# A mixture-of-experts and Mamba kernel: new order of an expert's chunks, normalisation moved to ScalarE, the last chunk's back end by token halves

## Chip, cores and metric

One NeuronCore of a Trainium2 chip runs the kernel. The metric is device time in microseconds of one execution, median over runs; lower is better. Engines in the tables: PE is TensorE (PEld its weight loads), DVE VectorE, ACT ScalarE, POOL GpSimd, SP SyncE.

## The reference, cut to what matters

```python
x = x + 0.5 * ffn(layernorm(x))          # 4096 tokens of 256 values
x = x + attn(layernorm(x))
x = x + 0.5 * ffn(layernorm(x))

def ffn(h):                               # 8 experts, top 2, capacity 640 for each of the two choices
    probs = softmax(h @ gate_w.T + gate_b); topk_prob, topk_idx = top_k(probs, 2)
    for c in range(2):                    # a token behind the capacity is dropped
        pos = place of the token among those of its expert; keep = pos < CAP
        hmid = relu(xb @ W1[e] + b1[e])   # 256 -> 1024
        y += (hmid @ W2[e] + b2[e])[token] * (prob * keep)

def attn(x):                              # Mamba, 512 inner channels, 16 states, 2 sequences of 2048
    x = x + mamba(rmsnorm(x))
    h = square(relu(rmsnorm(x) @ c_fc_w.T))
    return x + h @ c_proj_w.T

def mamba(xn):
    x_in, z = split(xn @ in_proj_w.T)
    u = silu(causal_conv4(x_in) + conv_b)
    dt_low, B, C = split(u @ x_proj_w.T); dt = softplus(dt_low @ dt_proj_w.T + dt_proj_b)
    h[t] = h[t-1] * exp(dt[t] * A) + dt[t] * u[t] * B[t];  y[t] = sum_s(h[t] * C[t]) + u[t] * D
    return (y * silu(z)) @ out_proj_w.T
```

## The kernel before

The tokens stay in SBUF as `X`, 32 tiles of 128. The program is a chain of blocks with a barrier at each end: `route` for the first expert layer, `experts`, `mamba`, `route` and `experts` for the second. Inside a block each engine has a program written out by hand, and semaphores join them, so an engine's order is the order of its code.

**route.** In the first layer X comes in four quarters. VectorE takes each quarter's `statistics`, GpSimd the power that gives the reciprocal deviation (`rstd`) and, for some quarters, `shift`. TensorE turns the tokens and makes the gate's logits; ScalarE copies both from PSUM. VectorE then selects two experts a token for each half of the tokens (`chosen(0)`, `chosen(1)`), with exponentials by ScalarE in the middle of each. The normalised tokens are made in eight groups of four tiles: `norm(g)`, groups 0 to 4 on VectorE, 5 to 7 on ScalarE. SyncE stores each group to `xrows` in DRAM, then issues the loads of the first weights, the copies of X into `sums`, the small columns of weights (`halves`), and the second bias. Then slots and tables are made (`hot`, `inblock`).

**experts.** Each expert has up to 1280 rows, in five chunks (parts) of 256, so 40 chunks a layer, two experts a turn `i`. Parts 2 to 4 are computed only when the expert has that many rows (`if_taken`); where one isn't, its gathers, row splits, bias and scatters are still done. For each chunk GpSimd gathers the rows (two indirect DMAs of 128), TensorE turns them (L629), ScalarE and VectorE split them into a high and a low float (`xh`, `xl`), TensorE makes the product up in four pairs (48 products, L654), VectorE adds the bias, ScalarE and VectorE split the relu (`hh`, `hl`), TensorE makes the product down (48 products, L672), VectorE takes it from PSUM (L790), scales it, and GpSimd scatters it with two indirect DMAs that add (L583). In a step TensorE turns chunk c+2, makes up of c+1, then down of c. In steps 1 to 4 of an expert the next expert's weights are split, 1.2 us a step on VectorE. At the start TensorE makes `WARM` small bf16 products that nobody reads, behind the first indices.

**mamba.** Eight chunks of 512 tokens. `front` makes a chunk's inputs: T (turned rows), x (in projection), c (convolution of four channel tiles), xp (x projection), dt, sp (softplus), z. `turn` is the scan: 32 steps of two channel tiles, with two VectorE scans and one GpSimd product `dB` each; what belongs to the next chunk's front and the last chunk's back is hung into the steps by tables. `back` is out projection (`out`), squares (`sq`), root (`v`), scaled rows (`hr`), turned rows (`hT`), the forward layer (`fc`, `q`) and its projection (`pj`). A join (`out`, `pj`) is an identity product of 512 columns and eight products. In the tables all these share two PSUM banks. The first chunk's front runs alone ahead of the scan, the last chunk's back alone behind it, step by step over the whole chunk, and beside it VectorE and GpSimd make the second routing's statistics (`row_statistics`), normalised rows and selection: a `power` on GpSimd stands ahead of the back end's `v`. In the first front, channel tiles 2 and 3 are convolved by VectorE (`first_convolved`), 0 and 1 by TensorE with diagonal matrices.

## Time and profile before

| what | value |
|---|---|
| median of 3 runs | 1924.44 us (1921.66 to 1924.93) |
| profiled execution | 1920.51 us |
| its span, first to last instruction | 1918.7 us |
| mean granted TensorE clock | 0.925 of full |
| busy: PE, DVE, POOL, ACT | 1663.3, 1594.3, 1346.2, 1010.1 us |

Busy time is a sum over stages that have different limits. A "wait" row names who waited, for whom, the total, how often and the longest. In a timeline row the first number is the start, the second the time to the end of the last merged instruction, and the bracket the idle time before it with its releaser. Matmuls of fp32 stand in the profile twice, and they overlap, so their starts tell more than their lengths.

### The profile page before, as it was taken

The page shows a single profiled execution, that of the slowest core. Times are in us where ns is not written, and L with a number is a line of the kernel's source. Part 1 is how long each engine was busy: PE and PEld are TensorE (multiplying, and loading weights), DVE is VectorE, ACT ScalarE, POOL GpSimd, SP SyncE. Part 2 cuts the span into 40 slices and gives each one's busy share as a digit, 9 for nine tenths or more (in the row PEclk, how much of TensorE's full clock was granted, in tenths as well). Part 3 has the DMA queues.
Part 4 walks back from the last instruction along what each step waited for, and adds up shares of the span by engine and source line. Part 5 has one row for each costly group of instructions (what it writes and reads, how often), then busy time and mean ns, then how long its engine had stood idle before and what let it go on. Part 6 is the DMA issues. An engine that isn't in the chain of part 4 may idle for free. (4 is left out here: it accounts for less than half of the span.)

```text
span 1918.7 us, 31529 instructions
## 1 busy us (share of the span) xinstructions
PE 1663.3 (87%) x10960; PEld 1387.0 (72%) x10960; DVE 1594.3 (83%) x2694; ACT 1010.1 (53%) x1716; POOL 1346.2 (70%) x847
## 2 busy tenths in 40 slices
PE   6599999995777798989888899888795799999996
PEld 5599999994345556656565666656773699999996
DVE  7777777665699999999999999999996677677764
ACT  3433333331476768787776878777552533333331
POOL 2356555556498899998989999898951366565555
PEclk9699999997889799999989999999797799999998
DMA  5744444332544444443544444444424744443341
GB/s 179 191 122 93 81 94 90 80 70 32 196 140 170 144 153 151 148 163 129 173 133 152 156 154 141 146 161 148 153 67 131 189 89 98 90 91 81 80 72 22
DMA packets 161101, 237.62 MB, mean 124 GB/s; under 512 B 29482, under 2 KB 85408, under 8 KB 160416
## 3 DMA queue, kind: packets, MB, share of 16 engines
q1 hardware_dynamic: 130208, 198.84, 31.6%
q0 software_dynamic: 30720, 36.53, 11.6%
q8 instruction: 102, 1.67, 0.4%
q14 instruction: 71, 0.58, 0.1%
HBM read 202.57 MB, written 38.34 MB: 126 GB/s over the span
## 5 line engine op out<-in xcount | busy, mean ns | idle before, releaser
L1588 POOL TENSOR_TENSOR m_dB<-m_DTU,m_BC 128x1024 f32<-128x1024 f32 x256 | 601.8, 2367 | 42.4 <-DVE m_HS L1714 40.6
L1714 DVE TENSOR_TENSOR_SCAN PS<-PS,m_ST,m_dB 128x512 f32<-128x512 f32 x400 | 496.8, 1274 | 14.6 <-POOL m_dB L1588 14.0
L1331 ACT ACTIVATE PS<-m_DT,m_A 128x512 f32<-128x512 f32 x512 | 332.3, 682 | 160.2 <-DVE m_ST L1730 159.7
L1306 PEld LDWEIGHTS PS<-keep_ident,m_G 128*128 128x128 f32 x2048 | 254.7, 150 | 89.6 <-issue 55.1
L1306 PE MATMUL PS<-keep_ident,m_G 128*128 128x128 f32 x2048 | 284.6, 288 | 17.7 <-DVE m_G L1721 15.9
L713 ACT ACTIVATE e_hh<-e_u 128x512 fp32r<-128x512 f32 x252 | 156.2, 633 | 265.5 <-DVE e_u L771 258.8
L654 PE MATMUL PS<-e_xh,e_wh 128*128 128x256 f32 x1008 | 290.0, 288 | 3.0 <-DVE e_xl L750 3.0
L654 PE MATMUL PS<-e_xl,e_wh 128*128 128x256 f32 x1008 | 284.2, 282 | 0.0
L654 PE MATMUL PS<-e_xh,e_wl 128*128 128x256 f32 x1008 | 284.2, 282 | 0.0
L672 PE MATMUL PS<-e_wh,e_hh 128*128 128x256 f32 x1008 | 281.3, 279 | 0.0
L672 PE MATMUL PS<-e_wl,e_hh 128*128 128x256 f32 x1008 | 280.3, 278 | 0.0
L672 PE MATMUL PS<-e_wh,e_hl 128*128 128x256 f32 x1008 | 279.9, 278 | 0.0
L1721 DVE TENSOR_TENSOR m_G<-PS,m_BC 128x512 f32<-128x512 f32 x400 | 266.2, 672 | 7.0 <-PE PS L1306 6.9
L577 POOL DMA_INDIRECT e_xin<-xrows,e_gix x160 | 196.4, 1227 | 57.9 <-issue 44.2
L583 POOL DMA_INDIRECT out<-e_ysb,e_six x80 | 135.1, 1689 | 139.0 <-DVE e_ysb L795 121.3
L583 POOL DMA_INDIRECT sums<-e_ysb,e_six x80 | 136.3, 1703 | 131.4 <-DVE e_ysb L795 111.9
L790 DVE TENSOR_TENSOR e_ysb<-PS,layer_b 128x512 f32<-128x512 f32 x80 | 55.2, 690 | 170.5 <-PE PS L672 168.2
L654 PEld LDWEIGHTS PS<-e_xh,e_wh 128*128 128x128 f32 x1008 | 193.6, 192 | 3.7 <-issue 3.6
L654 PEld LDWEIGHTS PS<-e_xl,e_wh 128*128 128x128 f32 x1008 | 193.9, 192 | 0.0
L654 PEld LDWEIGHTS PS<-e_xh,e_wl 128*128 128x128 f32 x1008 | 193.2, 192 | 0.0
L672 PEld LDWEIGHTS PS<-e_wl,e_hh 128*128 128x128 f32 x1008 | 189.3, 188 | 0.0
L672 PEld LDWEIGHTS PS<-e_wh,e_hh 128*128 128x128 f32 x1008 | 189.2, 188 | 0.0
(262 smaller groups left out, 3169.2 us busy)
## 6 DMA issues: line engine op xcount, KB each, us to landing
m_BC<-bc_rows SPq DMA_DIRECT2D x512, 256.0 KB, 3.8
layer_raw<-w SPq DMA_DIRECT2D x64, 512.0 KB, 3.8
xrows<-r_xn SPq DMA_DIRECT2D x9, 512.0 KB, 3.5
keep_X<-x SPq DMA_DIRECT2D x4, 1024.0 KB, 9.6
sums<-keep_X SPq DMA_DIRECT2D x4, 1024.0 KB, 11.0
out<-keep_X SPq DMA_DIRECT2D x4, 1024.0 KB, 11.1
keep_X<-sums SPq DMA_DIRECT2D x3, 1024.0 KB, 15.2
e_xin<-xrows,e_gix POOLq DMA_INDIRECT x160, 3.2
```

What stands on the lines that cost most here:

```text
L577: G.indirect_dma_start(out=xin[:, c % CPE, t, :], out_offset=None, in_=xrows, in_offset=column(gix, c, t), bounds_check=last_token, oob_is ...
L583: G.indirect_dma_start(out=sums, out_offset=column(six, c, t), in_=ysb[:, c % CPE, t, :], in_offset=None, compute_op=ALU.add, bounds_check ...
L654: last = M(PS[:, B_S1 + pair, m * CH:(m + 1) * CH], a, r, start=(n == 0), stop=(n == len(terms) - 1))
L672: last = M(PS[:, B_Y + c % 2, t * D:(t + 1) * D], a, r, start=(n == 0), stop=(n == len(terms) - 1))
L713: A(hh[:, c % 2, 2 * pair:2 * pair + 2, :], u[:, pair, :, :], ACT.Relu).then_inc(hh_ok, 1)
L790: V.tensor_tensor(ysb[:, c % CPE, :, :], PS[:, B_Y + c % 2, :].rearrange("p (t d) -> p t d", t=CHT), b2.unsqueeze(1).to_broadcast([P, CHT, ...
L1306: last = M(PS[:, B_Y + j, ts], G[:, m % NG, j, ts], C["ident"][:, :], is_transpose=True, start=False, stop=(s == DS - 1 and m == n and a = ...
L1331: return nc.scalar.activation(out, in_, func, **kw)
L1588: G_.tensor_tensor(dB[:, at % NDB, :, :], DTU[:, es, :], BC[:, s % NBC, 0:1, :].to_broadcast([P, 2, CT]), ALU.mult).then_inc(dB_ok, 1)
L1714: V.tensor_tensor_scan(HS[:, on_pool_before(n) % 2, :] if on_pool(n, j) else state(n, j), state(n, j), dB[:, (k * STEPS + n) % NDB, j, :], ...
L1721: V.tensor_tensor(G[:, n % NG, j, :], state(n, j), BC[:, s % NBC, 1, :], ALU.mult).then_inc(g_ok, 1)
```

## The change

It has six parts.

1. `route`: only groups 1 and 3 are normalised by VectorE. ScalarE makes 0 and 2 between its copies in quarters 1 and 2, and 4 to 7 behind the second exponentials; the first exponentials stand behind the last quarter's first copies. GpSimd makes `shift` for all quarters. SyncE stores in the order 1, 0, 3, 2, 4 to 7.
2. `experts`: the part that a position computes is given by a table, (0, 1, 3, 2, 4) for the first expert of a layer and (3, 0, 4, 2, 1) for the others. The row count of the next expert is read one chunk earlier.
3. `experts`: GpSimd gathers two chunks further ahead (`LEAD`), and `down` waits for `hl` pair by pair instead of for all four.
4. Warm products: 72 instead of 40 in each expert layer, with 18 more behind the first transposes; 44 at the start of `mamba`, behind the first statistics.
5. First front of `mamba`: VectorE convolves tiles 2, 3 and 1, TensorE only 0; the x projection adds its terms in the order 2, 3, 0, 1, each as its tile is ready.
6. The last chunk's back end (`tail`): each step by two halves of 256 tokens, over eight PSUM banks.

Parts 1 to 3:

```diff
-        ON_ACT = (5, 6, 7)
+        ON_DVE, ON_ACT = (1, 3), (0, 2, 4, 5, 6, 7)
+        STORED = (1, 0, 3, 2, 4, 5, 6, 7)
...
                 statistics(0)
                 statistics(1)
-                norm(0)
                 norm(1)
                 statistics(2)
-                norm(2)
                 norm(3)
                 statistics(3)
                 dve.wait_ge(gb_in, 16)
                 chosen(0)
-                norm(4)
                 chosen(1)
...
-        WARM = 40
+        WARM = 72
+        LEAD = 2
+        FIRST_ORDER, ORDER = (0, 1, 3, 2, 4), (3, 0, 4, 2, 1)
+
+        def part(i, c):
+            return (FIRST_ORDER if (i, c // CPE) == (0, 0) else ORDER)[c % CPE]
...
-            j = c % CPE
+            j = part(i, c) % CPE
             if j < 2:
                 return work()
             eng.sem_inc(passed, 1)
-            with eng.If(rows > j * CH):
+            with eng.If(known[2 * i + c // CPE] > j * CH):
...
-                pe.wait_ge(hl_ok, i * (TURN * FP) + (c + 1) * FP)
+                pe.wait_ge(hl_ok, i * (TURN * FP) + c * FP + 1)
...
                     for n, (a, r) in enumerate(terms):
+                        if t == 0 and n % 6 == 0:
+                            pe.wait_ge(hl_ok, i * (TURN * FP) + c * FP + n // 6 + 1)
```

Parts 5 and 6, TensorE's side; ScalarE's and GpSimd's `tail` follow the same halves, with GpSimd's root(0), power(0), root(1), power(1):

```diff
-        ON_VECTOR = [("c", 2), ("c", 3)]
+        ON_VECTOR = [("c", 2), ("c", 3), ("c", 1)]
...
+        TAIL_ITEMS = [("out", 0, 0), ("out", 1, 1), ("hT", 0, 4), ("fc", (0, 0), 5), ("fc", (0, 1), 3), ("hT", 1, 4),
+                      ("fc", (1, 0), 0), ("fc", (1, 1), 1), ("pj", 0, 5), ("pj", 1, 3)]
...
+            def tail():
+                k = MCH - 1
...
+                for h in range(2):
+                    tail_joined("out", h, W_OUT, lambda e: T3[:, e:e + 1, :], XP[:, 2 * h:2 * h + 2, :])
+                pe.wait_ge(kept, MCH * STEPS)
+                tail_turned(0)
+                wait_read(pe, MCH, ("dt", 1), ("z", 3))
+                logits(5, PS[:, R_L[5], :]).then_inc(r_l, 1)
+                pe.wait_ge(r_xT, 1)
+                tail_forward(0)
+                tail_turned(1)
+                logits(6, PS[:, R_L[6], :]).then_inc(r_l, 1)
+                tail_read(pe, "out", 1)
+                tail_forward(1)
+                for h in range(2):
+                    pe.wait_ge(q_ok, k * 2 + h + 1)
+                    pe.wait_ge(xa_ok, k * 2 + (h + 1 + XA0))
+                    tail_joined("pj", h, W_PJ, hid, X[:, bass.ds(k * CTT + 2 * h, 2), :])
```

ScalarE in the first routing, from the third quarter's copies of turned rows (`r_xnT`) on; `r_lg<-PS` are logits, `r_lg<-r_lg` the exponentials, `r_xn` the normalised groups. Before:

```order
L381 ACTIVATE r_xnT<-PS 128x1024 x2
L384 ACTIVATE r_lg<-PS 128x32 x2
L369 ACTIVATE r_lg<-r_lg 128x128
L375 ACTIVATE r_xn<-keep_X,r_small 128x256 x4
L381 ACTIVATE r_xnT<-PS 128x1024 x2
L384 ACTIVATE r_lg<-PS 128x32 x2
L369 ACTIVATE r_lg<-r_lg 128x128
L375 ACTIVATE r_xn<-keep_X,r_small 128x256 x8
```

The same engine in the changed kernel, from the second quarter's copies on:

```order
L378 ACTIVATE r_xnT<-PS 128x1024 x2
L372 ACTIVATE r_xn<-keep_X,r_small 128x256 x4
L385 ACTIVATE r_lg<-PS 128x32 x2
L378 ACTIVATE r_xnT<-PS 128x1024 x2
L372 ACTIVATE r_xn<-keep_X,r_small 128x256 x4
L385 ACTIVATE r_lg<-PS 128x32 x2
L378 ACTIVATE r_xnT<-PS 128x1024 x2
L366 ACTIVATE r_lg<-r_lg 128x128
L385 ACTIVATE r_lg<-PS 128x32 x2
L366 ACTIVATE r_lg<-r_lg 128x128
L372 ACTIVATE r_xn<-keep_X,r_small 128x256 x16
```

Between the third and the fourth quarter's copies stand now only logits and one normalised group made ahead of them; four groups stand at the end.

TensorE behind the last scan, from the gated rows (`m_YT`) on; `m_XP` with `m_MW,m_TH` is `out`, `keep_gate` are logits, `m_XR` turned rows, `m_hT` forward, `keep_X` with `m_MW,m_TH` is `pj`. Before:

```order
L1177 MATMUL PS<-keep_ident,m_YT 128x128 x8
L1234 MATMUL PS<-m_XP,keep_ident 128x512
L1237 MATMUL PS<-m_MW,m_TH 128x256 x8
L1234 MATMUL PS<-m_XP,keep_ident 128x512
L1237 MATMUL PS<-m_MW,m_TH 128x256 x8
L1258 MATMUL PS<-keep_gate,m_XI 128x8 x8
L1258 MATMUL PS<-keep_gate,m_xrT 128x8 x8
L1242 MATMUL PS<-keep_ident,m_XR 128x128 x8
L1246 MATMUL PS<-m_hT,m_MW 128x512 x8
L1234 MATMUL PS<-keep_X,keep_ident 128x512
L1237 MATMUL PS<-m_MW,m_TH 128x256 x8
```

And in the changed kernel, from the second join of `out`:

```order
L1312 MATMUL PS<-m_XP,keep_ident 128x512
L1315 MATMUL PS<-m_MW,m_TH 128x256 x8
L1323 MATMUL PS<-keep_ident,m_XR 128x128 x4
L1294 MATMUL PS<-keep_gate,m_XI 128x8 x8
L1332 MATMUL PS<-m_hT,m_MW 128x256 x8
L1323 MATMUL PS<-keep_ident,m_XR 128x128 x4
L1294 MATMUL PS<-keep_gate,m_xrT 128x8 x8
L1332 MATMUL PS<-m_hT,m_MW 128x256 x8
L1312 MATMUL PS<-keep_X,keep_ident 128x512
L1315 MATMUL PS<-m_MW,m_TH 128x256 x8
```

The turned rows and the forward products come in two halves, and the two groups of logits, which stood together ahead of them, now stand between: one behind each half's turned rows.

## Rows read from the trace of the kernel before

**Rows 1.** Windows: busy time of each engine, TensorE's granted clock, DMA share, GB/s.

```profile
75.00:456.00 381.00, 370.97 (x3176) 369.67 (x3174) 274.57 (x506) 129.74 (x195) 224.75 (x167) 0.98 0.41 87
526.00:1423.00 897.00, 784.12 (x3838) 545.88 (x3838) 876.88 (x1183) 663.80 (x1144) 826.87 (x425) 0.93 0.44 149
```

**Rows 2.** The page's costliest groups: count, then busy us, mean ns, idle before.

```profile
L713 ACT ACTIVATE e_hh<-e_u 128x512 fp32r<-128x512 f32 x252 | 156.2, 633 | 265.5 <-DVE e_u L771 258.8
L654 PE MATMUL PS<-e_xh,e_wh 128*128 128x256 f32 x1008 | 290.0, 288 | 3.0 <-DVE e_xl L750 3.0
L654 PE MATMUL PS<-e_xl,e_wh 128*128 128x256 f32 x1008 | 284.2, 282 | 0.0
```

**Rows 3.** Waits of TensorE from 75 to 470 us: total, times, longest.

```profile
PE PS L629 <- DVE e_xl L750: 6.0, 2, 3.0
...
PE PS L629 <- DMA e_xin<-xrows,e_gix: 2.5, 1, 2.5
```

**Rows 4.** Window behind layer 0's first pair of left-out chunks: TensorE busy, granted clock, DMA.

```profile
124.90:132.30 7.40, 7.40 (x52) 0.77 0.79 205
```

**Rows 5.** Timeline of VectorE and GpSimd at the end of both expert layers.

```profile
455.52 0.69 DVE L790 TENSOR_TENSOR e_ysb<-PS,layer_b 128x512 f32<-128x512 f32 x1 [3.90 <-PE PS L672]
...
470.68 1.56 POOL L583 DMA_INDIRECT sums<-e_ysb,e_six  x1 [0.31 <-issue]
...
1899.96 0.69 DVE L790 TENSOR_TENSOR e_ysb<-PS,layer_b 128x512 f32<-128x512 f32 x1 [3.88 <-PE PS L672]
...
1903.95 1.54 POOL L583 DMA_INDIRECT out<-e_ysb,e_six  x1 [0.30 <-issue]
...
1911.37 1.54 POOL L583 DMA_INDIRECT out<-e_ysb,e_six  x1 [0.30 <-issue]
```

**Rows 6.** Scatters (L583) from 466 to 472 us, all of chunks left out.

```profile
DMA to landing us min/median/max: 2.7/2.7/2.7
```

**Rows 7.** Scatters (L583) from 1893 to 1898 us, of a computed chunk.

```profile
DMA to landing us min/median/max: 3.7/4.0/4.2
```

**Rows 8.** Timeline of ScalarE and VectorE in the first routing.

```profile
30.48 2.06 ACT L375 ACTIVATE r_xn<-keep_X,r_small 128x256 f32<-128x256 f32 x4
...
34.77 1.38 DVE L225 TENSOR_SCALAR r_xn<-keep_X,r_small 128x256 f32<-128x256 f32 x4
...
39.23 0.29 DVE L260 TENSOR_TENSOR r_lg<-r_lg,r_small 128x128 f32<-128x128 f32 x1 [3.07 <-ACT r_lg L384]
```

**Rows 9.** Timeline of SyncE's queue, its last issue in the first routing.

```profile
61.20 5.56 SPq L200 DMA_DIRECT2D layer_b<-b  x1
```

**Rows 10.** Waits of SyncE's queue up to 80 us.

```profile
SPq L204 <- DMA xrows<-r_halves: 5.9, 1, 5.9
SPq L109 <- PEq L109: 1.6, 1, 1.6
```

**Rows 11.** Windows with L654 alone: TensorE and weight loads busy, granted clock, DMA.

```profile
83.70:88.60 4.90, 4.89 (x24) 4.89 (x24) 0.54 0.44 91
88.60:91.80 3.20, 3.01 (x26) 2.82 (x24) 1.00 0.77 80
```

**Rows 12.** Timeline of VectorE and GpSimd in the first front of mamba.

```profile
497.77 0.49 DVE L1667 TENSOR_SCALAR m_U<-m_XI,m_mc 128x512 f32<-128x512 f32 x1 [4.78 <-ACT m_XI L1331]
...
500.54 0.48 DVE L1667 TENSOR_SCALAR m_U<-m_XI,m_mc 128x512 f32<-128x512 f32 x1
...
520.61 1.23 DVE L1675 TENSOR_TENSOR m_DT<-m_DT,m_XR 128x1024 f32<-128x1024 f32 x1 [2.73 <-ACT m_XR L1331]
...
518.02 2.90 POOL L1525 TENSOR_TENSOR m_tk<-m_tk,m_mhalf 128x16 f32<-128x16 f32 x1 [1.21 <-DVEq L1648]
...
523.25 11.60 POOL L1588 TENSOR_TENSOR m_dB<-m_DTU,m_BC 128x1024 f32<-128x1024 f32 x5
```

**Rows 13.** Timeline of TensorE and VectorE in the last back end.

```profile
1427.72 3.62 PE L1237 MATMUL PS<-m_MW,m_TH 128*128 128x256 f32 x16
...
1467.29 0.75 DVE L1748 BATCH_NORM_STATS2 m_SZ<-keep_X 128x6 f32<-128x256 f32 x2 [3.56 <-ACT keep_X L1331]
```

More of the change, by code:

```diff
@@ L183, in _ @@
                 sp.dma_start(C["b1"][:, :], b1).then_inc(setup_sem("b1_in"), 16)
-                for g in range(NG):
+                for g in STORED:
                     if g in ON_ACT:
@@ L591, in step @@
             def step(i, c, first=False, last=False):
-                if not (last and c + CPE >= TURN):
-                    gp.wait_ge(picked, i * TURN + (c + 1))
-                    gp.sem_inc(carried, 1)
-                    gather(i, c + CPE)
+                for ahead in range(LEAD + 1) if first and c == 0 else (LEAD,):
+                    read = c + ahead
+                    if not (last and read + CPE >= TURN):
+                        gp.wait_ge(picked, i * TURN + (read + 1))
+                        gp.sem_inc(carried, 1)
+                        gather(*((i, read + CPE) if read + CPE < 2 * TURN else (i + 1, read + CPE - TURN)))
                 if c % CPE == 0:
@@ L678, in _ @@
             turn(0, 0, first=True)
+            for _ in range(WARM // 4):
+                M(PS[:, B_Y + 1, 0:P], C["onesb"][:, :], C["upper"][:, :], start=True, stop=True)
             up(0, 0, first=True)
             def step(i, c, last):
-                if c % CPE == 0:
-                    rows[0] = rows_of(pe, i, c // CPE)
+                next_rows(pe, i, c, rows)
                 if not (last and c + 2 >= TURN):
@@ L1066, in run @@
             last_yz()
-            for p in BACK:
-                between(p)
-                back(p, MCH - 1, 1)
+            tail()
         def items(engine, n, k, par, has_front, has_back, front, back, rows=lambda p: None):
@@ L1157, in _ @@
             M = nc.tensor.matmul
+            pe.wait_ge(var_ok, 1)
+            for _ in range(WARM):
+                M(PS[:, B_H, 0:P], C["onesb"][:, :], C["upper"][:, :], start=True, stop=True)
             pe.wait_ge(w_in, 16)
@@ L1207, in front @@
                     pe.wait_ge(w_in2, 16)
-                    pe.wait_ge(u_ok, k + 1)
-                    for e in range(EK):
-                        last = M(bank(p, k, XPR), weights(W_XP, XPR, e, 0, XPR), U[:, par, e, :], start=(e == 0), stop=(e == EK - 1))
+                    order = (2, 3, 0, 1) if is_first(k) else range(EK)
+                    if not is_first(k):
+                        pe.wait_ge(u_ok, k + 1)
+                    for at, e in enumerate(order):
+                        if is_first(k) and ("c", e) in ON_VECTOR:
+                            pe.wait_ge(conv_silu, ON_VECTOR.index(("c", e)) + 1)
+                        elif is_first(k):
+                            wait_read(pe, k, ("c", e))
+                        last = M(bank(p, k, XPR), weights(W_XP, XPR, e, 0, XPR), U[:, par, e, :], start=(at == 0), stop=(at == EK - 1))
                 elif kind == "dt":
@@ L1272, in rows, with tail_joined @@
                 last.then_inc(written(p, MCH), 1)
-            def between(p):
-                if p == ("g", 2):
-                    for d in range(DK):
-                        last = rows_turned(6, d, PS[:, R_T[6] + d, :])
-                    last.then_inc(r_T, 1)
-                elif p == ("hT", 0):
-                    wait_read(pe, MCH, ("dt", 1), ("z", 3))
-                    logits(5, PS[:, R_L[5], :]).then_inc(r_l, 1)
-                    pe.wait_ge(r_xT, 1)
-                    logits(6, PS[:, R_L[6], :]).then_inc(r_l, 1)
+            def tail_joined(kind, h, at, src, rows):
+                out = tail_bank(kind, h)
+                M(out, C["ident"][:, :], rows.rearrange("p t d -> p (t d)"), start=True, stop=False)
+                for t in range(2):
+                    for e in range(EK):
+                        last = M(out[:, t * D:(t + 1) * D], src(e)[:, 0, (2 * h + t) * P:(2 * h + t + 1) * P],
+                                 weights(at, D, e, 0, D), start=False, stop=(t == 1 and e == EK - 1))
+                last.then_inc(f_w, 1)
@@ L1308, in turn @@
                         last.then_inc(g_read, 1)
-            run(pe, turn, front, back, lambda: None, between)
+            run(pe, turn, front, back, lambda: None, tail)
             for h in range(2):
-                wait_read(pe, MCH - 1, ("pj", h))
+                tail_read(pe, "pj", h)
                 if h == 0:
@@ L1512, in _ @@
+            run(act, turn, front, back, lambda: None, tail)
             for h in range(2):
@@ L1564, in power, with tail, root @@
                                  ALU.pow).then_inc(r_pow, 1)
-            def between(p):
-                if p == ("v", 0):
-                    power(0)
-                    power(1)
+            def tail():
+                k = MCH - 1
+                def root(h):
+                    own = ssq[:, 2 * h:2 * h + 2]
+                    gp.wait_ge(sq_ok, k + h + 1)
+                    G_.tensor_tensor(own, own, eps[:, 0:2], ALU.add).then_inc(v_ok, 1)
+                    gp.wait_ge(v_ok, k + h + 1)
+                    G_.tensor_tensor(own, own, mhalf[:, 0, 0:2], ALU.pow).then_inc(rs_ok, 1)
+                root(0)
+                power(0)
+                root(1)
+                power(1)
+                for h in range(2):
+                    tail_read(gp, "out", h)
+                    x = X[:, bass.ds(k * CTT + 2 * h, 2), :]
+                    G_.tensor_tensor(x, x, XP[:, 2 * h:2 * h + 2, :], ALU.add).then_inc(xa_ok, 1)
             def weigh(k, n):
@@ L1599, in last_products @@
                         weigh(MCH - 1, n)
-            run(gp, turn, front, back, last_products, between)
+            run(gp, turn, front, back, last_products, tail)
             power(2)
@@ L1662, in first_convolved @@
                 dve.wait_ge(tail_ok, 1)
-                for n in range(2, EK):
+                for n in (e for _, e in ON_VECTOR):
                     wait_read(dve, 0, ("x", n))
```

165 lines of the change are left out of this document (122 added, 43 removed), and 2 rows, old and new, of the table base.

## Prediction

> **What bounds the kernel now.** I read the stages first, then who waited for whom inside them, then single rows. The two expert layers are bound by TensorE: from 75 to 456 us it is busy 370.97 of 381 us at a granted clock of 0.98. The scan from 526 to 1423 us is bound by VectorE, busy 876.88 of 897 us [rows 1]. The change leaves the steady part of both as it is: the same products, scans and transfers per chunk. What it can win lies in the seams: the first routing, the first chunk of each expert layer, the places where chunks are left out, the end of each expert layer, and both ends of the mamba stage. So each seam is priced by what ends last in it.
>
> Which chunks are left out matters for most of it. ScalarE's row L713 stands 252 times, four to a chunk that is computed, so 63 of the 80 chunks run [rows 2]. The lengths of the steps between TensorE's transposes (L629) show which: in layer 0 part 4 of experts 1 and 3, parts 3 and 4 of experts 0 and 6, parts 2 to 4 of expert 7; in layer 1 the same, but expert 7 leaves out only 3 and 4.
>
> **Chunks left out (c).** Where two neighbours are left out, TensorE has only transposes to do and waits for the split of the next rows: two waits of 3.0 us in layer 0 [rows 3], and two such in layer 1. Behind the first of them the clock is granted at 0.77 over 7.4 us of work, so some 1.6 us more is lost [rows 4]; one of the two in layer 1 shows the same, the others do not. The new order (3, 0, 4, 2, 1) puts computed chunks between parts 3 and 4, so four stalls of 3.0 us and two slow stretches of some 1.6 us go. Three things come back. Expert 7 of layer 0 leaves out parts 4 and 2, which are neighbours now: one wait stays, about 1.9 us, since the weight split of 1.2 us inside the old waits is missing in the last expert. A computed chunk between two that are left out has no other products behind which VectorE can make its low halves. That would cost some 2 us each, but the products down now start on the first pair and wait pair by pair; I take 0.3 us for each of six places, and 0.6 us for the last chunk of layer 0. Layer 0: -7.6 + 1.9 + 1.5 = -4.2. Layer 1: -7.6 + 0.9 = -6.7. **Sum -10.9**, bounds -15 and -5. The added waits themselves: in the products up, where each pair has a wait already, the term that begins a pair lasts 288 ns and the next 282 [rows 2]. 1008 times 6 ns over 252 waits is 24 ns a wait, so three more in each of 63 chunks cost at most 4.5 us. I take nothing, since these rows hold the slow first chunk too, and keep 4.5 as the bound.
>
> **Ends of the expert layers (d).** In layer 0 VectorE takes the last computed chunk from PSUM at 455.52. Then GpSimd issues eight scatters, six of them for chunks that are left out, the last from 470.68 to 472.24. In layer 1 it is 1899.96 and 1912.91. A chunk's own two scatters end 5.5 us after VectorE's read (1903.95 plus 1.54 against 1899.96) [rows 5]. In the new order the last position is always part 1, which is computed, so only these 5.5 us follow TensorE: 16.7 becomes 5.5 in layer 0, 12.95 becomes 5.5 in layer 1. Against it: a scatter that writes nothing lands in 2.7 us [rows 6], one that writes in 4.0 [rows 7], and issues some 0.3 longer. Layer 0: -11.2 + 1.6 = -9.6. Layer 1: -7.4 + 1.6 = -5.8. **Sum -15.4**, bounds -18 and -12.
>
> **First routing (a).** Three groups of four normalisations, 1.38 us each, leave VectorE for ScalarE, two of them ahead of its first selection. ScalarE's exponentials and its norm(5) (30.48, 2.06 us) stood ahead of the last turned rows, and so VectorE got its last logits only at 39.23, after 3.07 us of idle [rows 8]. Now the last quarter's copy comes first: it ends near 29.3, and the logits are there near 32.5. VectorE's first selection is held for its exponentials to about 29.65, one us sooner than before, and ends at 33.85, where the second starts: 5.4 us sooner. But the stage has a second chain. SyncE's last issue ended at 66.76 [rows 9], its wait for the small weight columns lasted 5.9 us more, to 72.6, and then it waited 1.6 us for the others [rows 10]. This chain hangs on the last normalised group, as all stores are issued before the sums. ScalarE makes that group behind the second exponentials, which come 5.4 sooner, but with two more groups of 2.06 ahead of it: 1.3 sooner. So SyncE ends at 71.3 and the stage, before at 74.2, with it: **-2.9**, bounds -1.3 and -5.4.
> The Trainium skill (Trainium Architecture — The Big Picture, The five engines, in one table) says that ScalarE is not for simple arithmetic, VectorE being up to about three times as fast per element. The row here shows a factor of 1.5, so the measurement decides. An estimate from that page's factor: four groups of 4.1 us behind the second exponentials would end 8 us later than mine, and the stage would cost 5 us instead of giving 2.9.
>
> **First chunk of each layer (b).** The warm products now number 72, with 18 more behind the first transposes. Before, the 40 ended 2.5 us ahead of the gathered rows [rows 3], and the first 24 products ran at a granted clock of 0.54 in 4.89 us; the next 24, with transposes, took 3.0 at full clock [rows 11]. So 2.2 us go, and 0.4 in the first transposes: **-5.2** for both layers. 72 products at the slow rate last about as long as the gather, so they delay nothing much. Bounds +1 (clock not raised, warm products late) and -6.5. VectorE's second pair of weight splits still ends before the second chunk's rows, so its chain moves along.
>
> **Front of mamba (e).** A third channel tile on VectorE costs 2.77 us (497.77 to 500.54). It takes c1 from TensorE, so the x projection ends some 4.4 us sooner. But VectorE still has three statistics blocks between its convolutions and the first sum of DT at 520.61, and GpSimd's power at 518.02 for 2.90 us hangs on the last of them, with the first dB at 523.25 behind four factors [rows 12]. All of this moves back by 2.77, of which some 1.4 returns, since two of GpSimd's factors took a us each beside VectorE's sums and now run alone: +1.35. If the 44 warm products raise the clock for the x products, these are 2.9 us earlier, and the front gains 1.5. I take **0**, with these two as bounds.
>
> **Last back end (f).** Before, the power of the row statistics stood ahead of the squares' root, out(1) waited for a bank, the whole chunk passed from step to step, and VectorE got the last rows at 1467.29. A join is 3.62 us of products and 0.9 for its identity term [rows 13]. By halves: out(0) and out(1) end at 1431.3 and 1435.85; squares, root and scale of the first half pass under out(1), and scaled rows stand at 1437.4. Transposes and logits(5) last to 1440.0, forward(0) to 1443.6, transposes and logits(6) to 1446.1, forward(1) to 1449.7, both joins to 1458.7, the copy to 1459.4: 7.9 sooner. Price: logits(6) come behind forward(0), so VectorE's selection starts 0.5 us later, and ScalarE's exponentials stand ahead of its next forward copy, 0.3 us; VectorE has reached the last statistics by 1457.5, so neither is on the chain. **-7.8**, bounds -9 and -4.
>
> **Sum.** -2.9 - 5.2 - 10.9 - 15.4 + 0 - 7.8 = -42.2. The profiled execution took 1920.5 (span 1918.7), which gives 1878.3; the median of the runs lies 3.9 above it: 1882. A difference of 0.2%, 3.8 us, is about what a measurement of this kernel can tell from none.
>
> **Rivals.**
> *Clock and stores.* The warm products don't hold the full level (the first 40 had lost it before their rows came [rows 11]) and the routing ends on its stores. Without b, without the 3.2 us of slow stretches in c, and with a at -1.3: -32, or 1892. Chance 0.2.
> *Every seam at its good bound:* the routing's transfers shrink with its chain, the x products find the full clock, left-out chunks cost nothing: -50, or 1874. 0.12.
> *The order does not do what it says.* If each left-out chunk still lets TensorE run dry, c is 0, and if the last scatters wait for one another's landing at the end of the layers, d halves: -24, or 1901. For it: every double left-out place shows its wait; against it: no wait of TensorE for a single left-out chunk stands beside them [rows 3]. 0.08.
> *GpSimd's power shuts VectorE out.* The sum of DT would begin behind the power, at 523.75, and the first dB at 526.3, 3.0 later than before instead of 0: 1885. Before, the sum began 0.3 us before the power ended and took 1.23 us as its neighbour did [rows 12]. 0.05. The Trainium skill (SBUF — State Buffer, SBUF: two separate sides) states this as a lock on a shared port pair, held for a whole instruction.
> *Slower: the finer waits open a bubble in every chunk.* TensorE is the bound through both layers, so each of the 63 computed chunks pays in full. From 42.2 / 63 = 0.67 us a chunk, 0.22 a wait, the gain is gone; at 0.3 a wait the time is 1939. The begun pairs bound it at 0.024 [rows 2]. 0.03. Within 0.2% of before: 0.02.
> The forecast itself has 0.5, with a range of 1877 to 1888. The whole range reaches into the neighbours: 1873 to 1897. All but the last two cases are faster: 0.95.
>
> **What would show it.** Right: no wait of 3.0 us on e_xl, but one near 2 in layer 0; two scatters behind TensorE's last product in each layer; VectorE's last logits of the routing without idle before them, and SyncE the last to end that stage; the first 24 products in 2.7 us; VectorE's last statistics of the mamba stage 7.8 us nearer to its last scan. Wrong: a first dB that lies later behind layer 0's last scatter than 51 us by more than 3; products down with gaps at each pair; more than one slow stretch in a layer.

## The result, and the profile after

The changed kernel takes 1879.6 us (median of four runs, 1878.3 to 1883.6) against 1924.4 for the kernel before: ratio 0.977, 95% interval 0.976 to 0.979. The forecast was 1882 with a range of 1873 to 1897. The profiled span falls from 1918.7 to 1877.9, by 40.8 us; the medians differ by 44.8, because the profiled execution of the kernel before took 3.9 less than its median. The ledger below cuts both traces at the same events, so its rows add up to the 40.8. "Read" is VectorE taking a chunk's result from PSUM.

| stretch | before | after | gain | forecast |
|---|---|---|---|---|
| a: start to first turned rows | 81.21 | 77.23 | 4.0 | 2.9 |
| b: first to third turned rows, both layers | 10.62 + 11.02 | 8.19 + 8.15 | 5.3 | 5.2 |
| c: from there to the read of the last computed chunk, layer 0 | 363.69 | 361.51 | 2.2 | 4.2 |
| c: the same, layer 1 | 375.25 | 370.04 | 5.2 | 6.7 |
| d: from that read to the mamba stage; to the end | 22.65; 18.74 | 12.36; 12.23 | 16.8 | 15.4 |
| e: start of mamba to first dB | 45.08 | 43.61 | 1.5 | 0 |
| scan, first dB to last product | 898.65 | 899.80 | -1.2 | 0 |
| f: to the last statistics | 45.39 | 38.32 | 7.1 | 7.8 |
| from there to the first turned rows of layer 1 | 46.40 | 46.46 | -0.1 | 0 |

The waits of TensorE in layer 0 (78 to 465 us; columns: total, how often, longest). Two waits of 3.0 us on e_xl stood here [rows 3]; one of 2.4 is left, at expert 7. Its row names VectorE's branch past a left-out chunk (L551), which VectorE reaches right behind its split of the rows:

```profile
PE PS L668 <- DVEq L551: 2.4, 1, 2.4
PE PS L668 <- DVE e_xl L765: 0.5, 1, 0.5
```

The page's groups of the products. In the products down the first group holds the products that begin a pair, a quarter of its 1008. Its mean is 281 ns where the other terms take 278, and it has 0.2 us of idle time in all. Before, it was 279 and 278. In the run with the old order below, which keeps the pair waits, it is 279 again, so the waits by themselves cost nothing that can be seen:

```profile
L688 PE MATMUL PS<-e_wh,e_hh 128*128 128x256 f32 x1008 | 283.3, 281 | 0.2
L688 PE MATMUL PS<-e_wl,e_hh 128*128 128x256 f32 x1008 | 280.5, 278 | 0.0
```

The end of layer 0, from GpSimd's timeline (start, length, bracket: the idle time before). Behind VectorE's last read, at 446.93, only two scatters begin and not eight [rows 5], once the one that began at 446.87 is over:

```profile
449.07 1.57 POOL L595 DMA_INDIRECT sums<-e_ysb,e_six  x1 [0.64 <-issue]
450.94 1.56 POOL L595 DMA_INDIRECT sums<-e_ysb,e_six  x1 [0.30 <-issue]
```

Windows of the start of layer 0: the first 24 products run at the full granted clock in 2.9 us, where they took 4.89 at 0.54 [rows 11]:

```profile
79.30:82.25 2.95, 2.91 (x25) 2.94 (x26) 2.51 (x3) 1.06 (x2) 2.41 (x2) 1.00 0.33 52
82.25:85.42 3.17, 3.17 (x30) 3.17 (x29) 1.88 (x5) 0.90 (x2) 2.56 (x3) 1.00 0.54 120
```

The first routing: SyncE's waits, and the timeline of VectorE and GpSimd. The second selection starts at 32.72 without idle time, 6.5 us sooner than before [rows 8]. SyncE then ends the stage with its wait for the small columns, and GpSimd's first indices stand at 70.56 (before, 74.62):

```profile
SPq L205 <- DMA xrows<-r_halves: 6.2, 1, 6.2
```

```profile
32.72 0.29 DVE L261 TENSOR_TENSOR r_lg<-r_lg,r_small 128x128 f32<-128x128 f32 x1
...
70.56 0.19 POOL L577 COPY e_gix<-layer_token 128x10 uint32<-128x10 uint32 x1 [26.53 <-POOLq L109]
```

The last back end, TensorE's timeline and a window. The same 16 forward products take 5.39 us for the first half of the tokens and 3.69 for the second, and the granted clock of the first stretch is 0.69:

```profile
1418.04 0.63 PE L1323 MATMUL PS<-keep_ident,m_XR 128*128 128x128 f32 x4 [1.57 <-ACT m_XR L1408]
...
1420.21 5.39 PE L1332 MATMUL PS<-m_hT,m_MW 128*128 128x256 f32 x16
...
1427.95 3.69 PE L1332 MATMUL PS<-m_hT,m_MW 128*128 128x256 f32 x16 [0.23 <-ACT m_hT L1408]
```

```profile
1420.00:1425.50 5.50, 5.50 (x21) 4.53 (x21) 5.50 (x11) 1.41 (x3) 4.80 (x3) 0.69 0.61 191
```

### The profile page after: what moved, and what is told of

It is laid out like the page before. It is cut to its first block and busy times, and to the rows that moved or that the text cites. A ratio compares the mean times of both kernels' runs of the same rounds, so it can differ in the third digit from the quotient of the medians.

```text
span 1877.9 us, 31848 instructions
## 1 busy us (share of the span) xinstructions
PE 1657.1 (88%) x11110; PEld 1388.6 (74%) x11112; DVE 1591.0 (85%) x2686; ACT 1014.9 (54%) x1728; POOL 1341.7 (71%) x851
## 5 line engine op out<-in xcount | busy, mean ns | idle before, releaser
L1858 DVE TENSOR_TENSOR_SCAN PS<-PS,m_ST,m_dB 128x512 f32<-128x512 f32 x400 | 498.6, 1281 | 15.4 <-POOL m_dB L1732 14.8
```

What stands on the lines that cost most here:

```text
L1858: V.tensor_tensor_scan(HS[:, on_pool_before(n) % 2, :] if on_pool(n, j) else state(n, j), state(n, j), dB[:, (k * STEPS + n) % NDB, j, :], ...
```

## The experiments

Every kernel is the changed one with the edit shown. Where a ratio stands, it is against the kernel before. Gains and losses are read between the events of the ledger.

### The order of the chunks

```diff
-        FIRST_ORDER, ORDER = (0, 1, 3, 2, 4), (3, 0, 4, 2, 1)
+        FIRST_ORDER, ORDER = (0, 1, 2, 3, 4), (0, 1, 2, 3, 4)
```

> The changed kernel, but every expert computes its chunks in the order 0, 1, 2, 3, 4 again; finer waits, warm products and the rest stay. The profiled changed kernel has a span of 1877.9 us. By my ledger of the two traces the two expert layers gained 7.4 us between their third transposes and their last computed chunk, and 16.8 us behind it. Theory A, the order makes both: waits of 3.0 us on e_xl stand again at the doubled left-out places, eight and six scatters behind the last computed chunk; span about 1902. Rival B, a good part comes from reading row counts and gathering two chunks further ahead, and from the pair waits: the waits of 3.0 us stay away and only the end comes back, span about 1895.

Measured: 1905.2 us, ratio 0.991 (0.989 to 0.992), span 1904.0. TensorE's waits on e_xl at the left-out places of layer 0 are those of before:

```profile
PE PS L643 <- DVE e_xl L765: 6.0, 2, 3.0
PE PS L668 <- DVE e_xl L765: 0.5, 1, 0.5
```

Stretch c is 363.58 and 375.01 us, as before (363.69 and 375.25), and d is 22.48 and 18.61. So the order makes all of c and d, 23.5 us of the 26.1 between the spans; the rest lies in the first routing (1.2) and the scan (1.3). Theory A holds. Reading the row counts sooner, gathering further ahead and waiting pair by pair are worth nothing by themselves, and the pair waits cost nothing either: the group of products down that holds them takes 281.2 us here and took 281.3 before, and stretch c is as long as before to 0.3 us.

```diff
-        FIRST_ORDER, ORDER = (0, 1, 3, 2, 4), (3, 0, 4, 2, 1)
+        FIRST_ORDER, ORDER = (0, 1, 3, 2, 4), (0, 2, 3, 4, 1)
```

> The changed kernel with the order 0, 2, 3, 4, 1: the last position is computed, as in the change, but parts 3 and 4 (and 2 where it is left out) are neighbours again. The first expert of a layer keeps 0, 1, 3, 2, 4. Tells the end of a layer apart from the stalls. If the stalls are what the new order removes beside the end: layer 0 has one wait of 3.0 us at expert 6 and two at expert 7 in place of the one of 2.4, layer 1 one at expert 6 and one at expert 7; 9.6 us more, less 0.9 for isolated places that go, and up to 1.6 us for each slow stretch behind a wait: span 1886 to 1891, with the ends of both layers as short as in the change (18.9 less 0, the mamba stage starting 12.4 us behind VectorE's last read). Rival: the ends lengthen too, because the scatters of left-out parts queue up ahead of the last: then span above 1893.

Measured: 1895.0 us, ratio 0.986 (0.984 to 0.987), span 1893.7. The span is 2.7 us above the range of the first theory and in that of the rival, but not for the rival's reason: the ends are as short as in the change (12.32 and 12.48), so a computed last position is all that d needs. Stretch c is 371.64 and 374.14, 10.1 and 4.1 us longer. In layer 0 the expectation had 6.6 and up to 1.6 for each slow stretch. TensorE waits in four places, one at expert 6 and three at the three left-out neighbours of expert 7 (columns as above). The wait for the split of the weights (e_wl) was not foreseen, and behind the others the granted clock falls, to 0.79 over the 8 us behind the wait of expert 6 and to 0.70 from 440.6 to 452 us:

```profile
PE PS L643 <- DVE e_xl L765: 4.5, 2, 2.8
PE PS L668 <- DVEq L551: 2.9, 1, 2.9
PE PS L688 <- DVE e_wl L761: 2.1, 1, 2.1
```

### The wait for the low halves

```diff
-                pe.wait_ge(hl_ok, i * (TURN * FP) + c * FP + 1)
+                pe.wait_ge(hl_ok, i * (TURN * FP) + (c + 1) * FP)
...
-                        if t == 0 and n % 6 == 0:
-                            pe.wait_ge(hl_ok, i * (TURN * FP) + c * FP + n // 6 + 1)
```

> The changed kernel, but the product down waits for all four low halves at once, as before. Theory A: in places where TensorE has no products up of another chunk in between (left-out chunks on both sides, and the last chunk of each layer) it now stands until VectorE has made the fourth low half, about 2 us for each of six isolated places and two ends less what they cost already (0.3 to 0.6 us each): span 10 to 13 us longer, about 1889. Rival B: VectorE is early enough even there: within 1 us of 1877.9. Rival C: the pair waits cost 24 ns each in the ordinary chunk, so that taking them away gives back up to 4.5 us of this.

Measured: 1904.9 us, ratio 0.990 (0.988 to 0.992), span 1902.8. Stretch c is 13.6 us longer in layer 0 and 10.2 in layer 1: 23.8 us, about twice what theory A gave. The waits are where A put them, layer 0 first, then layer 1:

```profile
PE PS L686 <- DVE e_hl L789: 9.3, 4, 2.5
...
PE PS L686 <- DVE e_hl L789: 7.2, 3, 2.5
```

That is 16.5 us at seven places: six isolated ones and the last chunk of layer 0. In the change the same places cost 0.2 to 0.7 us each, read from the length of their steps. Some 7 us come on top of the waits, and the granted clock is the reason: over some 8 us it is 0.77 to 0.80 behind five of the seven waits and 1.00 behind two. The five steps lose 3.6 to 5.0 us against the change (the longest, of the last chunk, has a second slow stretch in it), the two others 2.1 and 2.4. Windows of two of them: the step with the first wait takes 10.38 us at a granted clock of 0.84, where the change takes 6.36 at 1.00: 2.5 us are the wait, and 1.5 the clock behind it. The other keeps the clock and loses 2.1 (6.56 in the change).

```profile
110.28:120.66 10.38, 7.88 (x55) 7.65 (x54) 5.86 (x12) 3.64 (x5) 8.07 (x7) 0.84 0.49 103
395.17:403.84 8.67, 6.35 (x54) 6.12 (x53) 4.80 (x11) 2.69 (x4) 6.55 (x6) 1.00 0.52 79
```

What follows: the order and the pair waits belong together. With the new order and the old wait, c is 11.4 and 5.0 us longer than before the change. With the old order the pair waits are worth nothing.

### The warm products

```diff
-        WARM = 72
+        WARM = 40
...
-            for _ in range(WARM // 4):
+            for _ in range(0):
...
-        WARM = 44
+        WARM = 0
```

> The changed kernel with 40 warm products in each expert layer, none behind the first transposes, none in the mamba stage. Theory A, the warm products hold the granted clock: the first 24 products of each layer take 4.9 us again instead of 2.7 and the two steps after the first transposes 10.6 and 11.0 us instead of 8.2, so 5.3 us more in the expert layers; in the mamba front the x products take 9.4 us instead of 7.1 and the first scan comes 2 to 3 us later. Span about 1886. Rival B: gathering further ahead made the first steps shorter and the clock is worth less: under 3 us in the expert layers.

Measured: 1888.7 us, ratio 0.982 (0.980 to 0.984), span 1889.4. First to third turned rows: 10.46 and 10.99 us, as before (10.62 and 11.02), so the warm products make all of b (5.1 us). From the start of mamba to the first dB it is 46.35 us, 2.7 more than in the change. The x products take 9.65 us there and 7.13 in the change:

```profile
479.50 9.65 PE L1222 MATMUL PS<-m_xrT,m_MW 128*128 128x512 f32 x16 [0.69 <-ACT m_xrT L1408]
```

```profile
473.52 7.13 PE L1222 MATMUL PS<-m_xrT,m_MW 128*128 128x512 f32 x16 [0.74 <-ACT m_xrT L1408]
```

The rest of the 11.5 us between the spans lies in the first routing (1.5), the scan (1.4) and stretch c (0.7), which this edit doesn't touch. Theory A holds for both places. Without warm products the front is 1.3 us slower than before the change (46.35 against 45.08), so something else in it costs time. The front has two more edits, the third channel tile and the order in which the x projection adds its terms; the next run takes the tile back.

### The front of the mamba stage

```diff
-        ON_VECTOR = [("c", 2), ("c", 3), ("c", 1)]
+        ON_VECTOR = [("c", 2), ("c", 3)]
...
+             (("c", 1), 3),
```

> The changed kernel with two channel tiles convolved by VectorE as before (2 and 3), and 0 and 1 by TensorE; the warm products of the mamba stage and the x projection in ready order stay. From the start of the mamba stage to the first dB: 45.08 us before, 43.61 in the change, 46.35 in the change without warm products. Theory A, the third tile costs 1.27 us (46.35 less 45.08) because VectorE's statistics and GpSimd's power behind them set the first dB: 42.3 now, 1.3 shorter than in the change. Rival B: TensorE's second convolution delays the x projection and with it DT: 43.6 or more. The earlier reading of which chain ends last is what it tests.

Measured (one profile): span 1875.8, first dB 41.40 us behind the start of the stage, 2.2 sooner than in the change, where nine profiles with three tiles lie between 43.5 and 43.9. With two tiles VectorE waits 1.14 us for ScalarE before the sum of DT, so ScalarE's side now ends last there. Rival B, which gave no gain at all, falls. Two rows of VectorE, the first of this kernel, the second of the change:

```profile
499.44 1.22 DVE L1819 TENSOR_TENSOR m_DT<-m_DT,m_XR 128x1024 f32<-128x1024 f32 x1 [1.14 <-ACT m_XR L1408]
```

```profile
499.27 1.29 DVE L1819 TENSOR_TENSOR m_DT<-m_DT,m_XR 128x1024 f32<-128x1024 f32 x1
```

With three tiles ScalarE has DT 5.2 us ahead of VectorE, which still makes statistics. The third tile is a loss, 2.2 us here. The new order of the x projection was not taken back, so what it gives is not shown. The scan is 898.8 us in this kernel and 899.0 to 901.2 in ten profiles with three tiles; before, it was 898.65. The nearest two are 0.2 us apart, so that a link with the tiles is not shown, and how they could lengthen the scan was not found.

The next kernel attacks the same wait from the other side:

```diff
-            for call in range(2, len(CALLS)):
+            for call in range(2, len(CALLS) - 1):
                 statistics(call, *CALLS[call])
             first_dt()
+            statistics(len(CALLS) - 1, *CALLS[-1])
...
+                        if is_first(k) and n == 3:
+                            factors(len(CALLS) - 1, *CALLS[-1])
```

> The changed kernel, but in the front of the mamba stage VectorE makes the sum and the product of the first DT ahead of its last statistics block, and GpSimd that block's factors behind the first four dB. In the change ScalarE has DT ready 34.8 us behind the start of the stage and VectorE starts its sum at 39.98, behind the statistics; with two tiles on VectorE the pair is 38.3 and 38.3, and the first dB stands at 41.40 instead of 43.61. Theory A, with three tiles on VectorE the statistics block of 4.9 us is all that stands between: sum at 35.1, first dB at 38.8, when GpSimd's power for the block before is done, first scan about 42.6 instead of 46.07, and nothing is given back, as VectorE waited there; span 1873 to 1875. Rival B: GpSimd's factors among the first dB delay the scan by 3.5 us, and the gain is gone.

Measured (one profile): span 1877.4. The first dB stands at 38.9 us, as worked out, 4.7 sooner than in the change. All of it is lost behind: the first scan comes 47.6 us behind the start of the stage (46.07 in the change). Rival B is not the reason, as GpSimd's factors come only at 511.4. The scan starts behind VectorE's small operations of the late statistics, and some of these stand while GpSimd makes dB. VectorE first, then GpSimd:

```profile
500.07 0.16 DVE L1784 TENSOR_TENSOR m_var<-m_st 128x8 f32<-128x8 f32 x1
500.16 2.32 DVE L1785 TENSOR_TENSOR m_var<-m_st 128x8 f32<-128x8 f32 x1
502.51 2.26 DVE L1786 TENSOR_SCALAR m_tk<-m_tk 128x8 f32<-128x8 f32 x1
504.80 0.17 DVE L1787 TENSOR_TENSOR m_var<-m_var 128x8 f32<-128x8 f32 x1
...
497.76 6.97 POOL L1732 TENSOR_TENSOR m_dB<-m_DTU,m_BC 128x1024 f32<-128x1024 f32 x3
```

An operation of 0.17 us takes 2.32, as long as one dB (6.97 / 3), and the next one waits out another dB. With the last dB over, 0.17 is back.

### The first routing

In the first of three kernels the small columns are issued right behind the normalised groups; in the second the copies into `sums` go ahead of group 4; the third has the routing of before.

```diff
+            if x_dram is not None:
+                weights_out()
             for q in range(4):
                 load_quarter(sp, W1, W2, raw, 0, q)...
```

```diff
                 for g in STORED:
+                    if g == 4:
+                        copy_sums()
```

> The changed kernel, but in the first routing SyncE issues the small weight columns right behind the normalised groups, ahead of the loads of weights and the copies of X into sums. In the changed kernel VectorE's last table stands at 67.2 us, SyncE's wait for these columns ends at 70.1, and the first indices at 70.56 (71.65 to 72.03 in four variants with the same routing). Theory A, SyncE's queue of stores ends the stage: the columns land some 15 us earlier, the wait for them goes, and the indices stand at 68.2 to 68.7, 2.0 to 3.5 us sooner; span about 1875.5. Rival B: something else (the copies into sums, b2's 1 MB, the barrier) ends within 0.5 us of it, and the stage ends at 70 or later.

> The changed kernel, but SyncE issues the four copies of X into sums (4 MB) ahead of the last four groups of normalised rows instead of behind the weights. SyncE waits 11.5 us there for ScalarE, and the DMA engines move nothing from 30 to 35 us, while from 45 to 70 us their share is 0.95 to 1.23. With the small columns issued first (the earlier run) the stage did not end sooner, as the copies then ended last. Theory A, the transfers as a whole end the stage, and filling the hole takes this chain away: first indices at 68.0 to 69.0, about 1 us behind VectorE's last table at 67.2, against 70.56 to 72.06 in seven profiles; span 1874 to 1877. Rival B: the stores of the last groups and the weights now queue behind the copies and end as late as before: 70 or later.

> The changed kernel with the whole routing stage as before (groups 0 to 4 normalised by VectorE, the old order of ScalarE and of the stores). Before, the first indices stood at 74.62; with the change at 70.56 in one profile and between 70.69 and 72.47 in seven others of the same text (one of them with another order of SyncE's queue). Theory A: the change of the routing is worth 2.2 to 4.1 us, first indices at 74.6 here, and nothing else moves; span about 1881. Rival B: part of the four microseconds is how one execution differs from another: indices at 73 or sooner.

Measured (one profile each): first indices at 72.06, 68.61 and 75.31 us, spans 1881.0, 1875.5 and 1883.9. Theory A of the first falls. The small columns no longer end last, but the copies into `sums` do, in SyncE's waits:

```profile
SPq L109 <- DMA sums<-keep_X: 6.5, 1, 6.5
```

So the place of the small columns in the queue was not it; the transfers as a whole are what is left. The second run shows it. Windows of 30 to 35 us, the change first (the last two columns are the DMA share and GB/s): the hole is filled. Two rows of the second run show VectorE's table of tokens and, 0.9 us behind it, the first indices; VectorE's last operation of the stage ends between them, at 68.25.

```profile
30.00:35.00 5.00, 1.29 (x12) 1.10 (x10) 4.14 (x16) 1.19 (x4) 0.00 (x0) 0.99 0.00 0
```

```profile
30.00:35.00 5.00, 1.80 (x17) 1.60 (x15) 4.18 (x15) 0.88 (x4) 0.00 (x0) 1.00 1.04 338
```

```profile
67.71 0.24 DVE L331 TENSOR_TENSOR layer_token<-layer_dest,r_masks 128x80 uint32<-128x80 uint32 x1
...
68.61 0.19 POOL L583 COPY e_gix<-layer_token 128x10 uint32<-128x10 uint32 x1 [24.08 <-POOLq L109]
```

The third run sizes term a. The old routing gives 74.62 and 75.31 in two profiles; the new one lies between 70.56 and 72.47 in nine, mean 71.4. So a is worth 3.6 us on average, and the 4.0 of the first profile is at its good end.

### The last back end

```diff
                 pe.wait_ge(kept, MCH * STEPS)
+                for _ in range(24):
+                    M(tail_bank("hT", 0)[:, 0:P], C["onesb"][:, :], C["upper"][:, :], start=True, stop=True)
                 tail_turned(0)
```

> The changed kernel with 24 small bf16 products that nobody reads in the gap of 1.57 us that TensorE has in the last back end ahead of its first turned rows (1416.5 to 1418.04). Behind that gap the clock was granted at 0.69 from 1420.0 to 1425.5 and the first half's forward products took 5.39 us, the second half's 3.69. Theory A, the gap (and the thin logits behind it) drops the clock, and the last back end is 7.1 us shorter than before instead of 7.8 for that reason: forward products of the first half in 3.7, VectorE's last statistics 36.6 us behind its last scan product instead of 38.32; span about 1876. Rival B: the slow stretch comes from the logits' thin products alone and stays: 38.3.

Measured (one profile): span 1876.8, last statistics 36.56 us behind the last scan product instead of 38.32. Theory A holds: the gap dropped the clock, and the thin logits behind it alone don't. TensorE's timeline and the window of the forward products, now at a granted clock of 1.00:

```profile
1416.06 1.50 PE L1349 MATMUL PS<-keep_upper,keep_onesb 128*128 128x128 bf16 x24
...
1419.90 3.70 PE L1332 MATMUL PS<-m_hT,m_MW 128*128 128x256 f32 x16
```

```profile
1420.00:1425.50 5.50, 5.50 (x37) 5.04 (x36) 5.50 (x11) 2.99 (x6) 4.56 (x3) 1.00 0.61 191
```

Of these 1.76 us, 0.8 are lost again behind them. From the last statistics to layer 1's first turned rows it takes 47.3 us here and 46.4 to 46.5 in every kernel without this edit; the last kernel below, which has it too, takes 47.2. Layer 1's first indices come 2.0 us sooner than in the change, but TensorE waits 1.61 us for the rows that they gather, and not 0.42. From 1479 to 1481 us, when the gather is issued, the DMA share is 0.56; in the change, at the same distance from its gather (1481 to 1483), it is 0.00. So other transfers, which did not move along, are likely what holds the gather up; no run tests it. TensorE's first turned rows, in the change and in this run:

```profile
1487.48 0.66 PE L643 MATMUL PS<-keep_ident,e_xin 128*128 128x128 f32 x4 [0.42 <-DMA e_xin<-xrows,e_gix]
```

```profile
1486.30 0.66 PE L643 MATMUL PS<-keep_ident,e_xin 128*128 128x128 f32 x4 [1.61 <-DMA e_xin<-xrows,e_gix]
```

### Gathering further ahead

```diff
-        LEAD = 2
+        LEAD = 0
```

> The changed kernel with gathers no further ahead than before (LEAD 0 instead of 2). In the prediction this edit has no term. Theory A, it only matters where steps are short (left-out chunks), where GpSimd's scatters and gathers of two chunks would fall into 6 us: up to 1 us at each of the eight left-out places of layer 0, span 0 to 5 us longer. Rival B: the gathers are needed: TensorE's transposes wait for DMA at each left-out place, over 10 us longer. Rival C: nothing, within 1 us.

Measured (one profile): span 1877.4. Stretch c is 361.23 us in layer 0 (361.51) and 369.56 in layer 1 (370.04). The edit is worth nothing that one profile can show, as rival C has it.

### The three findings together

The kernel holds three diffs from above: the copies into `sums` ahead of group 4, the 24 products in the last back end, and two tiles on VectorE.

> The changed kernel with the three edits that the runs point to: the copies into sums issued in SyncE's idle time, 24 small products in the gap of the last back end, and two instead of three channel tiles on VectorE in the first front. One by one they gave in the profiles: first indices at 68.61 instead of 71.4 (the mean of nine profiles of the changed routing), 1.76 us in the last back end, and 2.2 us at the first dB with about 0.7 more in the scan. If they add, 2.8 + 1.8 + 2.9 = 7.5 us: a span of 1871 to 1873 and a median near 1873, 0.973 to 0.975 of before. Rival: they overlap, as the granted clock or the phase of the products moves with every shift: 1876 or more.

Measured: 1873.4 us, ratio 0.974 (0.972 to 0.975), span 1871.6. First indices at 68.63, first dB 41.28 us behind the start of its stage, scan 898.51, last back end 36.57. Against the change that is 1.9 us at the indices, 2.3 at the first dB, 1.3 in the scan and 1.75 in the back end, less 0.7 lost behind it. The rest cancels, and the spans differ by 6.3. The time lies in the range that was expected, though two terms are smaller than there: the change's own profile has its first indices at the good end, and the loss behind the back end was not seen. The interval lies below that of the changed kernel (0.976 to 0.979), so this version beats both.

## Why the prediction was right

**The whole.** 42.2 us were forecast and the spans give 40.8. The terms are off by 0.1 to 3.5 us, in both directions, so part of the closeness is luck: a, d and e gave 4.0 us more than forecast, c, f and the scan 5.4 less. The forecast of 1882 rests on the 3.9 us between the profiled execution and the median before; the change showed no such distance (1879.7 and 1879.6).

**a.** The steps held: VectorE's last logits without idle time, SyncE last. Average 3.6, forecast 2.9. But the reason for SyncE's place was only half seen. The prediction hung its chain on the last normalised group; what ends it is the sum of the transfers behind, which an idle stretch of the DMA engines could have taken. ScalarE made four groups in a row in 7.96 us, 2.0 each as the row of before had it. The Trainium skill (Trainium Architecture — The Big Picture, The five engines, in one table) has ScalarE up to three times slower at simple arithmetic; the estimate made from that, a stage 5 us longer, does not hold here.

**b.** Right in size and cause: 5.3, and 5.1 of it goes with the warm products.

**c.** The mechanism was right, the size was not: 7.4 instead of 10.9. The stalls and slow stretches of left-out neighbours went as priced; what comes back is larger. The wait left at expert 7 is 2.4 and not 1.9 us. The isolated places cost 0.2 to 0.5 us in layer 0 as assumed, and 1.2 to 1.6 in all in layer 1 instead of 0.9. The rest is the pace of the products, below: more of them ran at the slower of two paces, some 2.5 us in both layers together. The order as such could not have won that. What the prediction priced well without seeing its weight is the pair waits: "some 2 us each" was 2.4, and a slower clock behind some of them would have made it 23.8 us in all.

**d.** 16.8 instead of 15.4, since the writing scatters cost 0.9 us more at each end and not 1.6. Of this price the 0.3 for the issue was misread: an issue takes 1.54 to 1.57 us whether its rows are written or not.

**e.** The forecast of 0 lay between two bounds, and the good one, 1.5, is what came. Both of its parts were real: a loss by the third tile (bound 1.35, measured 2.2 with warm products; the 1.27 without them holds the new order of the x projection too) and a gain by the clock (2.7 at the first dB; the x products gained 2.3 and not 2.9). The parts don't add up simply: with two tiles, the clock and the new order of the x projection give 3.7 us together. The chain was named rightly, VectorE's statistics; but the gain of the clock was kept out of the likeliest case. That GpSimd's power would shut VectorE out did not happen: the sum took 1.29 us beside it (before 1.23 [rows 12]).

**f.** 7.1 instead of 7.8. The step that failed is "forward(0) to 1443.6": it assumed the full clock, and behind the gap ahead of it the products took 1.7 us more, as behind the wait of [rows 4]. The other steps were 1.0 us shorter than forecast, which hid most of it. No run takes the halves, the eight banks or GpSimd's order back one by one, so which of them makes the 7.1 is not shown.

**Rivals.** No bubble in every chunk: with the old order and the pair waits, c was as long as before. The order did what it says. The clock held: it is 1.00 from 76 to 451 us and from 1486 to 1866.

## What to carry to other kernels

An order that puts skipped work between computed work removes one stall and makes another: ask what the neighbour was hiding, and split the wait on it in the same edit. Price a gap of TensorE at its length plus what follows at a lower clock: here 1.5 to 1.7 us behind some gaps of 1.6 to 3.0 and nothing behind others as long. A few products that nobody reads can fill one, but follow such a gain to the next block: here nearly half of it was lost again. Before blaming the last transfer in a queue, look for the stretch in which the DMA engines were idle.

## What the runs showed of the hardware that was not expected

**Two paces of the same products.** A step of 96 products and four transposes lasts either 11.34 to 11.36 or 11.74 to 11.76 us, at a granted clock of 1.00 in both, with no gap between products. Two neighbouring steps of the kernel before:

```profile
212.96:224.31 11.35, 11.35 (x102) 11.35 (x101) 8.34 (x15) 4.04 (x6) 5.90 (x4) 1.00 0.45 93
224.31:236.06 11.75, 11.75 (x102) 11.75 (x101) 8.26 (x15) 3.99 (x6) 5.83 (x4) 1.00 0.46 90
```

From start to start a product takes 113.3 or 117.8 ns, behind the first ones of a step. In most steps the pace is kept throughout and changes at the start; a few (11.58 us in layer 1 of the change, 11.63 and 11.68 in others) change inside. The number of slow steps hardly moves: in layer 0 it is 12 of 22 in ten of the eleven kernels with the new order and 11 in one; before, 12 of 26. Which steps are slow does move. With the same code in the expert layers, the change and the kernel with two tiles have different ones, so the text of the program does not settle it alone. What sets it stays open.

**VectorE stands behind GpSimd's products, but not behind its power.** In the kernel with late statistics, operations that take 0.17 us elsewhere took 2.32 and 2.26 beside dB. Beside a power of 2.90 us, which began at 499.26 in the change, the sum of DT took 1.29 and the product behind it (500.67) 1.23, both with two inputs in SBUF. The Trainium skill (SBUF — State Buffer, SBUF: two separate sides) states a lock on a shared port pair, held for a whole instruction, where VectorE is in a two-port mode, or has two SBUF inputs while GpSimd reads SBUF. For dB the trace agrees; for the power, whose inputs are in SBUF too, it doesn't.
